# Reordering the low parts of gelu, the norms and the score waits in a shifted-window transformer block on one core

## What is computed

```python
def ref(x, ...):                       # x: (16, 56, 56, 192) float32
    shortcut = x
    xn = layernorm(x, ln1_w, ln1_b)
    xs = jnp.roll(xn, shift=(-3, -3), axis=(1, 2))
    xw = windows_of_7x7(xs)            # 1024 windows of 49 tokens
    q, k, v = heads(xw @ qkv_w + qkv_b)           # 6 heads of 32
    attn = softmax(einsum('bhqd,bhkd->bhqk', q, k) * 32 ** -0.5)
    o = einsum('bhqk,bhkd->bhqd', attn, v) @ proj_w + proj_b
    x = shortcut + unroll(o)
    h = layernorm(x, ln2_w, ln2_b)
    h = gelu(h @ mlp_w1 + mlp_b1)                 # 192 -> 768, exact gelu
    return x + (h @ mlp_w2 + mlp_b2)              # 768 -> 192
```

## Time and profile before

| what | value |
|---|---|
| time, median of 3 runs | 3140.79 us (3136.73 to 3142.77) |
| the profiled execution's own time | 3139.02 us |
| its span, first to last instruction | 3137.2 us |
| mean granted TensorE clock | 0.991 |
| busy: PEld | 2877.8 us, 92% |
| busy: DVE | 2569.4 us, 82% |
| busy: ACT | 2276.2 us, 73% |
| busy: POOL | 1635.4 us, 52% |
| DMA, mean over the span | 25 GB/s |

### The profile page before, as it was taken

One profiled execution on the slowest core, in us unless ns is written; L12 is line 12 of the kernel. 1 busy time (PEld: TensorE's weight loads), 2 busy tenths in 40 slices (PEclk: granted clock), 3 DMA queues, 4 the chain that ended last, 5 costly groups with the idle time before them and its releaser, 6 DMA issues.

```text
span 3137.2 us, 114862 instructions
## 1 busy us (share of the span) xinstructions
PE 2988.8 (95%) x43446; PEld 2877.8 (92%) x43446; DVE 2569.4 (82%) x6418; ACT 2276.2 (73%) x4493; POOL 1635.4 (52%) x1934
## 2 busy tenths in 40 slices
PE   6999999999999999999999999999999999999997
PEld 5999999999999999999999999999999999999987
DVE  5788888888888888888888888888888888888873
ACT  3677777777777777777777777777777777777765
POOL 2455545555554555555455455555545555554543
PEclk8999999999999999999999999999999999999998
DMA  1010010001001000000100100010010001001000
GB/s 49 20 29 23 23 29 25 23 26 28 23 23 30 24 23 27 27 23 25 29 24 23 29 25 23 25 28 23 23 29 25 23 26 28 23 23 30 24 21 17
DMA packets 109333, 79.89 MB, mean 25 GB/s; under 512 B 7294, under 2 KB 108782, under 8 KB 109294
## 3 DMA queue, kind: packets, MB, share of 16 engines
q1 hardware_dynamic: 107682, 77.18, 9.1%
q10 hardware_dynamic: 1612, 2.16, 0.2%
HBM read 40.78 MB, written 38.54 MB: 25 GB/s over the span
## 4 chain that ended last, share of the span: by engine, by line
issue 41%; PE 22%; POOL 20%; ACT 8%; DVE 7%; ACTq 1%; POOLq 1%; DVEq 0%
POOL gl L393 11%; PE ps L842 9%; PE ps L839 6%; ACT g L682 4%; DVE z L439 4%; ACT gh L688 4%; PE ps L869 2%; PE ps L962 2%; POOL rs L376 2%; POOL zh L385 2%; POOL xb L366 2%; DVE qB L471 2%; POOL prob L278 1%; PE ps L810 1%; DVE yTb L569 1%
## 5 line engine op out<-in xcount | busy, mean ns | idle before, releaser
L393 POOL TENSOR_TENSOR gl<-g,gh 128x392 fp32r<-128x392 f32 x768 | 766.7, 1032 | 344.2 <-ACT gh L688 344.2
L278 POOL TENSOR_TENSOR prob<-prob,rcp 128x588 f32<-128x588 f32 x128 | 152.0, 1187 | 1070.2 <-DVE rcp L579 1070.2
L839 PE MATMUL ps<-zh,w 128*128 128x392 f32 x3072 | 699.9, 343 | 0.6 <-ACT zh L650 0.6
L839 PEld LDWEIGHTS ps<-zh,w 128*128 128x128 f32 x3072 | 551.0, 188 | 0.8 <-ACT zh L650 0.8
L682 ACT ACTIVATE g<-ps,biasf 128x392 f32<-128x392 f32 x768 | 396.8, 592 | 166.1 <-PE ps L839 166.1
L439 DVE TENSOR_SCALAR z<-x,mv,rs 98x192 f32<-98x192 f32 (+2 forms) x768 | 305.1, 465 | 226.5 <-issue 209.4
L839 PE MATMUL ps<-zh1c,wqkv 128*128 128x392 f32 x1536 | 362.1, 344 | 5.8 <-DVE zh1c L449 5.8
L748 ACT ACTIVATE oh<-ps 128x392 fp32r<-128x392 f32 x128 | 68.2, 533 | 401.0 <-PE ps L962 401.0
L688 ACT ACTIVATE gh<-g 128x392 fp32r<-128x392 f32 x768 | 355.6, 552 | 0.0
L842 PE MATMUL ps<-wqkv,zh 128*114 128x192 f32 x2048 | 291.4, 270 | 12.2 <-DVE prob L544 2.6
L842 PEld LDWEIGHTS ps<-wqkv,zh 128*114 128x114 f32 x2048 | 261.9, 184 | 31.8 <-issue 31.8
(11 more groups left out here) (110 smaller groups left out, 7293.6 us busy)
## 6 DMA issues: line engine op xcount, KB each, us to landing
xin<-in_x SPq DMA_DIRECT2D x128, 147.0 KB
out<-yo SPq DMA_DIRECT2D x128, 147.0 KB
xin<-in_x SPq DMA_DIRECT2D x128, 71.2 KB
out<-yo SPq DMA_DIRECT2D x128, 71.2 KB
xin<-in_x SPq DMA_DIRECT2D x128, 54.8 KB
out<-yo SPq DMA_DIRECT2D x128, 54.8 KB
xin<-in_x SPq DMA_DIRECT2D x128, 18.8 KB
out<-yo SPq DMA_DIRECT2D x128, 18.8 KB
```

The costliest lines, as they stand in the source:

```text
L393: pool.tensor_tensor(gl[:, m, :], g[:, m, :], gh[:, m, :].bitcast(F32), ALU.subtract)\
L839: last = pe.matmul(dst, cols(w, part), act_, start=(n == 0), stop=(n == 4))
```

## The change

- POOL makes gl chunks 0 to 2, then norm 2's root, then chunk 3 (`POOL_GL = 4`). Chunks 4 and 5 are made by DVE (`last_gelu_parts`), behind `stats1` and ahead of `low_parts1`, with a semaphore of their own that `mlp2` waits on.
- On DVE `apply1` moves ahead of the residual, and `narrow_result` ahead of `queries_45`.
- On POOL the wait for z2_done moves ahead of `pad_windows`, which so runs behind norm-2 z.
- The first half's score subtraction is two instructions, one for each PSUM bank (two heads' blocks of 294 columns), and `v` waits for each before it writes that bank. The counts of s_sub become three for a group.
- `TP` is turned to (4, 2): the first half of the probabilities' transposes waits for gelu's chunk 3, the second for the residual.
- Four iterations are written out at each end instead of five, so the loop covers 122.

```diff
--- before.py
+++ after.py
@@ -122,7 +122,8 @@
         Y = (6, 7)
         TY = (6, 7)
         T1 = 0
-        TP = (2, 4)
+        TP = (4, 2)
+        POOL_GL = 4
         PV = 2
         PROJ = (2, 3)
         OFFSETS = (7, 7)
@@ -180,6 +181,7 @@
         g_done = sem("g_done")
         gh_done = sem("gh_done")
         gl_done = sem("gl_done")
+        gl_last_done = sem("gl_last_done")
         y_done = sem("y_done")
         yT_ready = sem("yT_ready")
         yn_ready = sem("yn_ready")
@@ -248,15 +250,14 @@
                     lo += n * blocks
                     src = src + n * blocks
 
-        def iterations(eng, body, last=GROUPS - 4):
-
-
-            for i in range(5):
+        def iterations(eng, body, first=4, after=GROUPS - 2):
+
+            for i in range(first):
                 body(i, i % 2)
-            with eng.Fori(0, (last - 4) // 2) as j:
-                body(j * 2 + 5, 1)
-                body(j * 2 + 6, 0)
-            for i in range(last + 1, GROUPS + 2):
+            with eng.Fori(0, (after - first) // 2) as j:
+                body(j * 2 + first, 0)
+                body(j * 2 + first + 1, 1)
+            for i in range(after, GROUPS + 2):
                 body(i, i % 2)
 
         def attends(i):
@@ -385,10 +386,10 @@
                     last = pool.tensor_copy(spaced(spread), packed(tight).bitcast(F32))
                 last.then_inc(zpad_done, 1)
 
-            def gelu_parts(prev):
+            def gelu_parts(prev, chunks):
 
                 wait(pool, y_done, 1, prev - 1, 1)
-                for m in range(KC):
+                for m in chunks:
                     wait(pool, gh_done, KC, prev, m + 1)
                     pool.tensor_tensor(gl[:, m, :], g[:, m, :], gh[:, m, :].bitcast(F32), ALU.subtract)\
                         .then_inc(gl_done, 1)
@@ -403,15 +404,17 @@
                 if attends(i):
                     normalise(pool, i, 0)
                 if feeds(i):
-                    gelu_parts(i - 2)
+                    gelu_parts(i - 2, range(3))
                 if mixes(i):
                     rstd(mv2, ve2, rs2, mv2_done, ve2_done, rs2_done, i - 1, z2_done)
+                if feeds(i):
+                    gelu_parts(i - 2, range(3, POOL_GL))
                 if more(i):
+                    wait(pool, z2_done, 1, i - 1, 1)
                     pad_windows(i + 1)
                 if more(i + 1):
                     rstd(mv1, ve1, rs1, mv1_done, ve1_done, rs1_done, i + 2, z1_done)
                 if more(i):
-                    wait(pool, z2_done, 1, i - 1, 1)
                     add_proj_bias(i + 1, 1 - parity)
 
             iterations(pool, body)
@@ -541,9 +544,12 @@
                 peak, p = mx[:, slots], prob[:, slots, 0:TOK]
                 dve.tensor_reduce(peak, src, AX.X, ALU.max).then_inc(smax, 1)
                 wait(dve, smax, 2, i, part + 1)
-                dve.tensor_tensor(p.rearrange("p (r q) k -> p r q k", r=2), src,
-                                  peak.rearrange("p (r q) -> p r q", r=2).unsqueeze(3)
-                                      .broadcast_to([128, 2, TILES // 2, TOK]), ALU.subtract).then_inc(s_sub, 1)
+                p, peak = p.rearrange("p (r q) k -> p r q k", r=2), peak.rearrange("p (r q) -> p r q", r=2)
+                for banks in ((slice(0, 1), slice(1, 2)) if part == 0 else (slice(0, 2),)):
+                    n = banks.stop - banks.start
+                    dve.tensor_tensor(p[:, banks], src[:, banks],
+                                      peak[:, banks].unsqueeze(3).broadcast_to([128, n, TILES // 2, TOK]), ALU.subtract)\
+                       .then_inc(s_sub, 1)
 
             def residual(i, parity, half):
 
@@ -570,6 +576,14 @@
                                              blocks_of(yn[:, :], odd), ALU.add)
                 last.then_inc(yTb_ready, 1)
 
+            def last_gelu_parts(prev):
+
+                wait(dve, y_done, 1, prev - 1, 1)
+                for m in range(POOL_GL, KC):
+                    wait(dve, gh_done, KC, prev, m + 1)
+                    dve.tensor_tensor(gl[:, m, :], g[:, m, :], gh[:, m, :].bitcast(F32), ALU.subtract)\
+                       .then_inc(gl_last_done, 1)
+
             def row_sums(i, half):
 
                 wait(dve, p_exp, 2, i, half + 1)
@@ -598,6 +612,8 @@
                     row_sums(i, 0)
                     row_sums(i, 1)
                     normalise(dve, i, 1)
+                if more(i):
+                    apply1(i + 1, 1 - parity)
                 if mixes(i):
 
                     wait(dve, xb_done, 1, i - 1, 1)
@@ -605,13 +621,12 @@
                     wait(dve, z2_done, 1, i - 2, 1)
                     for half in range(2):
                         residual(i - 1, 1 - parity, half)
-                if more(i):
-                    apply1(i + 1, 1 - parity)
-                if mixes(i):
                     wait(dve, x2_done, 2, i - 1, 2)
                     norm_stats(x2[:, 1 - parity, :, :], st2, mv2, bn2, mv2_done, i - 1)
                 if more(i + 1):
                     stats1(i + 2, parity)
+                if feeds(i):
+                    last_gelu_parts(prev)
                 if not mixes(i) and attends(i):
                     low_weights_1()
                 if more(i):
@@ -626,10 +641,11 @@
                                       (z2[:, h, C + B:2 * C], 2 * h + 1, slice(0, A))]
                     wait(dve, t2_done, 1, i - 2, 1)
                     norm_apply(x2[:, 1 - parity, :, :], mv2, rs2, z2_pieces, i - 1, mv2_done, rs2_done, z2_done)
+                if feeds(i):
+                    narrow_result(prev)
                 if more(i):
                     queries_45(i + 1)
                 if feeds(i):
-                    narrow_result(prev)
                     result(prev, parity)
 
             iterations(dve, body)
@@ -689,7 +705,7 @@
 
             def exponential(i, half):
 
-                wait(act, s_sub, 2, i, half + 1)
+                wait(act, s_sub, 3, i, half + 2)
                 scores = half_of(prob, half)[:, :, 0:TOK]
                 act.activation(scores, scores, ACT.Exp, scale=SCALE).then_inc(p_exp, 1)
 
@@ -853,8 +869,9 @@
             def v(i):
 
                 wait(pe, zpad_done, 1, i, 1)
-                wait(pe, s_sub, 2, i, 1)
                 for p in range(PAIRS):
+                    if p % 2 == 0:
+                        wait(pe, s_sub, 3, i, p // 2 + 1)
                     last = project(ps[0:PAIR + 1, V + p // 2, 256 * (p % 2):256 * (p % 2) + C], zh1, zl1, wqkv,
                                    lambda w, part: w[:, part, 2 * C:3 * C],
                                    tokens=slice(2 * WIDE * p, 2 * WIDE * p + PAIR + 1))
@@ -892,7 +909,7 @@
                 wait(pe, zh2_done, 3, prev, 1)
                 for m in first:
                     if m == 0 and attends(prev + 2):
-                        wait(pe, s_sub, 2, prev + 2, 2)
+                        wait(pe, s_sub, 3, prev + 2, 3)
                     if m == 2 and attends(prev + 2):
                         wait(pe, v_ready, 1, prev + 2, 1)
                     chunk(m, (0, 1, 2), {2: [(zl2_done, 2, prev, 1)]})
@@ -911,7 +928,10 @@
                     pe.matmul(wide, w2l[:, k, :], gh[:, k, :], start=False, stop=False)
                     pe.matmul(narrow, w2s[:, k, :], gh[:, k, :], start=(k == 0), stop=False)
                 for k in range(KC):
-                    wait(pe, gl_done, KC, prev, k + 1)
+                    if k < POOL_GL:
+                        wait(pe, gl_done, POOL_GL, prev, k + 1)
+                    else:
+                        wait(pe, gl_last_done, KC - POOL_GL, prev, k + 1 - POOL_GL)
                     pe.matmul(wide, w2h[:, k, :], gl[:, k, :], start=False, stop=(k == KC - 1))
                     last = pe.matmul(narrow, w2s[:, k, :], gl[:, k, :], start=False, stop=(k == KC - 1))
                 last.then_inc(y_done, 1)
@@ -931,7 +951,7 @@
 
                 for half in range(2):
                     wait(pe, p_norm[half], 1, i, 1)
-                    if half == 0:
+                    if half == 1:
                         wait(pe, x2_done, 2, i - 1, 2)
                     elif feeds(i):
                         wait(pe, g_done, KC, i - 2, 4)
@@ -1023,7 +1043,7 @@
                     turn_probs(i)
                 if more(i):
                     wait(pe, z1_done, 1, i + 1, 1)
-                    wait(pe, s_sub, 2, i, 2)
+                    wait(pe, s_sub, 3, i, 3)
                     if feeds(i):
                         wait(pe, g_done, KC, prev, 2)
                     transposes1()
```

## The result

The changed kernel takes 2993.68 us (median of 4, 2990.98 to 2995.93) against 3141.61 (median of 4): a ratio of 0.9532, 95% interval 0.9515 to 0.9548. The forecast was 3009 with a range of 2990 to 3042. The profiled execution took 2994.5 us, with a span of 2992.4.

A forecast was written before the change was run, and what follows sets the result against it. PE, busy 95% of the span, bounds the kernel through its waits: 0.81 + 0.25 - 0.05 = 1.01 us per iteration, 127 us in all, plus 4.5 for the loop's ends, gives 3009 us; own range 2994 to 3026, stated 2990 to 3042.

The forecast's parts named there:

- The wait on yTb: PE's transposes of yTb wait for DVE; the whole 0.81 us per iteration was to go.
- held pieces: Norm-2 z on DVE: the piece that meets POOL's work takes 1131 ns, an undisturbed one 375.
- the late start behind the root: DVE's norm-2 z starts only when POOL's root ends, behind six gl chunks, after 1.67 us of idleness.
- The wait for the subtraction: PE's value projection `v` waits for DVE's score subtraction; splitting it was to gain all of 0.25 us per iteration.
- The new wait: PE's second half of the probabilities' transposes now waits for DVE's residual; 0.05 us per iteration charged, bounds 0 and 0.3.
- The loop's ends: Two written-out iterations move into the loop; 4.5 us gain taken, from 5.5 by the rows, with a bound of zero.
- The cost of gelu's chunks: Two gl chunks on DVE delay `low_parts1`, but PE's `qk` was to get it in time: cost zero.
- the worse order: POOL's chunk 3 comes between DVE's two gl chunks; `low_parts1` still ends 0.3 us before `qk` wants it.
- ACT's qA: Rival: qA is 0.1 to 0.3 us late for PE's scores, 3036 us in the middle; chance 0.10.
- the query projection: PE's `qk`, which needs `low_parts1`; the slow rival had it wait 1.65 us.
- the residual 0.10: Rival at the probabilities' second half: residual 0.76 us later as a piece of apply1 is held, 3092 us; chance 0.07.
- The slow rival: DVE's gelu low parts are held by POOL's root and chunk 3, net 0.6 us slower per iteration, 3211 us; chance 0.05.

The follow-up runs named there:

- no_gelu: The changed kernel with gelu's low parts as before (six chunks on POOL, then norm 2's root): 2992.4 us.
- e_gelu: The kernel before with one edit, norm 2's root between POOL's third and fourth chunk of gl and chunks 4 and 5 on DVE: 3120.4 us.
- u_scores: The changed kernel with the first half's score subtraction in one piece again: 3019.6 us.
- gl3: The changed kernel with three chunks of gl on DVE and three on POOL, none after the root: 2991.6 us.
- three: The changed kernel with gelu's low parts as before and POOL's copies ahead of norm-2 z again: 3003.1 us.

## Why the prediction was right, and where it was small

- **The wait on yTb, 0.81.** Right: gone, and nothing else took its place at L947. Two of its causes were read right (held pieces, and qB in front), and removing one of them takes all but 0.06. The third, the late start behind the root, is still there in no_gelu, and yTb is in time all the same. The forecast never asked which edit does it.
- **The wait for the subtraction, 0.25.** 0.30 by the table of parts. I let `v` start 0.17 behind the first transpose of the pair; it starts 0.11 behind it. The mean of the waits, 31.8 over 125, that I then took was low by as much.
- **The new wait, 0.05.** It is there, 0.10. The step was right: apply1 takes 1.24, the residual ends a moment after PE is ready, and PE's second half of the transposes stands for it in every iteration. It cost twice what I charged, within the bounds of 0 and 0.3. One part of the sum shows in the trace: PE's second half starts 0.15 behind the residual's end in each of 100 iterations, where I took 0.05 for this step from yTb's row.
- **What was overlooked.** From yTb's transposes to the scores PE needed 0.42 and needs 0.31. Before, it was 0.49 in every second iteration, the one in which the loop's branch (L256) stands behind the wait, and 0.36 in the others, where the two transposes of yTb start 0.15 apart instead of 0.11. With PE running on both are gone; that they are then hidden is my reading. This 0.11 could be read from the same rows that I used for the 0.81 and is not in the sum. So 0.81 + 0.25 - 0.05 = 1.01 was 0.82 + 0.30 + 0.11 - 0.10, less 0.02 elsewhere: 1.11. Over 126 iterations the difference is 12 of the 15 us by which the forecast was high.
- **The loop's ends, 4.5.** The difference between the two spans beyond the period is 5.3, but the loop's bounds aren't its cause: undone, they cost 0.4 us with intervals that overlap. The bound of zero was the right value, and that 4.5 comes near 5.3 is luck. What makes up the 5.3 isn't settled; starts and ends differ by some microseconds from kernel to kernel (66.6 to 71.9 us behind iteration 126 in the two tables above), with the clock of these stretches.
- **The cost of gelu's chunks, zero.** Right: `low_parts1` ended at 1212.34 with `qk` at 1212.68, a cover of 0.34 against 0.3 worked out, by the worse order. That DVE and POOL hold each other there was in the forecast; that both get longer, 0.93 or more and 1.44, was not. The Trainium skill ("SBUF — State Buffer", section "Who interferes with whom") has the later of two fully blocked. The chunks that came second, 1.40 and 1.44, fit that; DVE's first, which started 0.39 to 0.48 ahead of POOL's and still took 0.93 or more, doesn't, if POOL's chunk is what it met. It may be another thing: the first ends 0.53 to 0.56 behind the start of POOL's chunk wherever it started itself, 0.62 long with a start 0.08 ahead (e_gelu, medians), 1.28 long with a start 0.73 ahead (u_scores). In the last case it would have been over before POOL's chunk began. POOL's root was running, but in gl3, where no chunk follows the root, the first took 0.53 to 0.54 with 0.44 of it beside the root. So neither the chunk nor the root alone explains it, and what holds it stays open.
- **The rivals.** ACT's qA and the query projection set nothing, and the residual 0.10. The slow rival needed DVE to lose every turn, 4.0 us in all; both chunks took 2.25, and three take 1.49 where POOL has none behind its root (gl3).
- **The range.** 2993.7 lies at the lower end of the forecast's own range, 2994 to 3026. The stated range begins at 2990, and the working gives no reason for these 4 us; the 0.11 that the sum lacks is most of what took the time there.

What the forecast lacked was an order of need. Its working had each edit remove its own share, and the sum came out right because the change has all of them. Taken apart, the gains are about 95 us for yTb or the copies alone, and 11 for the copies where yTb is already ahead (three against no_gelu); 26 for the scores, in the changed kernel with the new order, and the same on the kernel before for another reason; 17 for gelu and root alone, and 0 in the changed kernel; 0 for the loop. They don't add up to the 148 of the whole. The order of norm-1 z alone wasn't run; without it the finished kernel loses 108.

## What to carry to other kernels

When one engine waits for another once per iteration, look for the cheapest thing in the last microsecond before the wait, such as a step that could stand behind it, or another engine's work that lengthens it; once the wait is gone, further edits to the same chain buy little. A gain upstream moves engines against each other: before an edit that makes PE earlier, see which operations of the others will then meet, as 0.3 us cost 0.95 here where it brought two of POOL's chunks onto norm-1 z. Undo each part of a bundle from the finished kernel as well as trying it alone: here the copies' move gave 96 us by itself and 11 where yTb already stood ahead of qB.

## What the runs showed of the hardware

- A subtraction of 392 columns with both operands in SBUF takes DVE 0.53 to 0.57 us, the same as with one in PSUM (0.57). POOL's root of four columns (1.02 us) beside it for 0.44 doesn't slow it where nothing follows the root (gl3). With POOL's subtraction of 392 columns behind the root, DVE's first takes 0.61 to 1.31 us, by how far ahead it starts (0.07 to 0.77; e_gelu, u_scores and the changed kernel), and its second 1.38 to 1.40, and POOL's takes 1.42 to 1.45 instead of 1.03.
- Norm pieces of 192 columns on DVE take 0.375 us alone; beside POOL's chunks four of them took 1.24 with none held, 2.00 with one, 2.68 to 2.78 with two.
- In the changed kernel the profile shows PE busy for all of the 2680.00 us from 170 to 2850, with a granted clock of 1.00, that is 2.4 GHz. The 0.10 that it waits for the residual in each iteration doesn't show there, only in the starts of its matmuls.
